# Expert stage of a graph and mixture-of-experts layer: opening with blocks listed from an early copy of the counts

## What is computed

```python
def gnn(x, adj, mask, W, b, a1, a2, att_b):
    h = x @ W + b
    att = sigmoid((h @ a1)[:, :, None] + (h @ a2)[:, None, :] + att_b) * adj * mask[:, :, None] * mask[:, None, :]
    att = att / (att.sum(-1, keepdims=True) + 1e-8)
    return (att @ h) * mask[:, :, None]

def ffn(x, gate_w, gate_b, w1, b1, w2, b2, gamma, beta):
    vals, idx = top_k(x @ gate_w + gate_b, 2)
    y_e = relu(x @ w1[e] + b1[e]) @ w2[e] + b2[e]          # for the two experts e of each token
    y = x + (softmax(vals) * y_e).sum()
    return layernorm(y) * gamma + beta

x = x + gnn(layernorm(x), ...)
x = x + ffn(layernorm(x), ...)
```

## Time and profile before

| | |
|---|---|
| median of 3 runs | 476.04 us (474.75 to 476.56) |
| the profiled execution, its own time | 477.23 us |
| span of the profiled execution | 475.5 us |
| busy: PE, DVE, ACT, POOL | 340.2, 313.2, 231.1, 324.4 us |
| scatters (L399), sends (L421) | 128 and 143 |
| first and last start of POOL's scatters | 48.28 and 211.60 us |
| first and last start of POOL's sends | 229.63 and 415.41 us |

### The profile page before, as it was taken

The page is one execution under the profiler, slowest core; times in us unless marked ns, Lnnn a source line. Parts: engine busy times, 40 slices in busy tenths (PEclk is TensorE's granted clock), DMA queues, the critical chain, the costliest instruction groups (busy, mean ns, idle before and its releaser), DMA issues.

```text
span 475.5 us, 11764 instructions
## 1 busy us (share of the span) xinstructions
PE 340.2 (72%) x2193; PEld 279.7 (59%) x2193; DVE 313.2 (66%) x1582; ACT 231.1 (49%) x608; POOL 324.4 (68%) x362
## 2 busy tenths in 40 slices
PE   2787988697778555103998989988889899058760
PEld 1666877687768454002877877777777788023220
DVE  3999898868968855701676666665555566118993
ACT  2767788788777364100333333333333335005663
POOL 6642777777777777660577777777777777705875
PEclk9998879969969955555999999999999999659995
DMA  7832445635444723595657777777777763179833
GB/s 206 280 106 63 146 157 173 203 110 210 158 156 156 266 102 111 178 257 178 200 163 223 234 206 228 218 216 219 220 223 226 210 197 103 37 277 291 274 108 110
DMA packets 61786, 87.96 MB, mean 185 GB/s; under 512 B 10343, under 2 KB 40973, under 8 KB 61604
## 3 DMA queue, kind: packets, MB, share of 16 engines
q1 hardware_dynamic: 32484, 44.87, 32.4%
q0 software_dynamic: 10720, 25.32, 14.8%
q10 hardware_dynamic: 18528, 17.19, 12.3%
HBM read 55.60 MB, written 32.72 MB: 186 GB/s over the span
## 4 chain that ended last, share of the span: by engine, by line
PE 24%; DVE 18%; ACTq 17%; issue 16%; ACT 9%; DMA 5%; POOL 5%; SPq 5%; DVEq 1%; POOLq 0%
PE psum L1190 6%; ACTq L553 6%; ACTq L272 5%; PE psum L1179 5%; ACTq L271 4%; ACT hid L558 4%; PE psum L1095 3%; DMA sorted_x<-xrow,rows 3%; PE psum L1113 3%; ACT z L582 3%; DVE st L654 2%; POOL sorted_x L399 2%; POOL token_y L421 2%; DVE xmid L718 1%; DVE rs L1010 1%
## 5 line engine op out<-in xcount | busy, mean ns | idle before, releaser
L421 POOL DMA_INDIRECT token_y<-yb,xb x143 | 143.4, 1003 | 60.4 <-issue 39.7
L399 POOL DMA_INDIRECT sorted_x<-xrow,rows x128 | 123.4, 964 | 42.0 <-issue 39.9
L558 ACT ACTIVATE hid<-psum,b_sb 128x256 f32<-128x256 f32 (+1 forms) x188 | 69.3, 419 | 140.4 <-PE psum L1179 63.4
L1190 PE MATMUL psum<-w_sb,hid 128*128 x572 | 83.3, 282 | 12.8 <-ACT hid L558 12.1
L1190 PEld LDWEIGHTS psum<-w_sb,hid 128*128 128x128 f32 x572 | 74.6, 191 | 22.4 <-issue 19.9
L1179 PE MATMUL psum<-xbT,w_sb 128*128 128x256 f32 (+1 forms) x376 | 81.9, 341 | 2.5 <-DVE xbT L955 2.2
L964 DVE TENSOR_TENSOR yb<-psum,b_bc 128x256 f32<-128x256 f32 x94 | 33.8, 360 | 63.1 <-PE psum L1190 50.2
L1179 PEld LDWEIGHTS psum<-xbT,w_sb 128*128 128x128 f32 x376 | 57.7, 193 | 8.2 <-DVE xbT L955 4.9
L969 DVE SCALAR_TENSOR_TENSOR yb<-yb,xb 128x128 f32<-128x128 f32 x143 | 46.6, 354 | 3.3
L1169 PE MATMUL psum<-ident_aug,xb 128*128 128x128 f32 x143 | 33.1, 288 | 21.8 <-DMA xb<-sorted_x 20.1
L955 DVE COPY xbT<-psum 128x256 f32<-128x256 f32 x94 | 33.2, 353 | 22.4 <-PE psum L1169 22.4
(11 more groups left out here) (159 smaller groups left out, 569.0 us busy)
## 6 DMA issues: line engine op xcount, KB each, us to landing
xb<-sorted_x SPq DMA_DIRECT2D x49, 258.0 KB
w_sb<-w_dram ACTq DMA_DIRECT2D x83, 128.0 KB
adj_in<-adj_dram SPq DMA_DIRECT2D x32, 256.0 KB
got<-token_y SPq DMA_DIRECT2D x16, 512.0 KB, 4.8
xb<-sorted_x SPq DMA_DIRECT2D x45, 129.0 KB
out_dram<-res ACTq DMA_DIRECT2D x16, 256.0 KB, 2.2
w_sb<-w_dram SPq DMA_DIRECT2D x27, 128.0 KB
xmid<-x_dram SPq DMA_DIRECT2D x6, 512.0 KB, 8.4
```

Source lines behind the costliest of these rows:

```text
L399: pool.indirect_dma_start(sorted_x, bass.IndirectOffsetOnAxis(ap=rows[:, slot, t, k:k + 1], axis=0), xrow[:, slot, k, t, :], None).then_in ...
L421: pool.indirect_dma_start(token_y, bass.IndirectOffsetOnAxis(ap=xb[:, q, t, TO:TO + 1].bitcast(I32), axis=0), yb[:, h, t, :], None, bounds ...
L558: last = act.activation(hid[:, u % RING, c, 0:n], psum[:, 2 + u % 2, c * BT:c * BT + n], ACT.Relu, bias=b1_sb[:, c, e])
L1190: last = mm(psum[:, 4 + u % 2, t * D:(t + 1) * D], hid[:, u % RING, c, t * P:(t + 1) * P], w2_sb[:, e, c * D:(c + 1) * D].rearrange("p a c ...
```

## The change

- The constants: `ORDER` is now 11 full units, then 15 times three one-tile units and a full one, then 23 full units. There are four lists of units: 17 full ones that lie wholly in what the first eight pairs wrote, 15 full ones of the middle, 17 full ones that are counted back from each expert's last row, and the 45 one-tile units.
- DVE copies `count` to `early` after the eighth pair. For this its loop is split: turns 4 to 9 in a loop, turns 10 and 11 written out with the copy between them, turns 12 and 13 in a loop of one pass.
- The table is computed from both copies: 44 operations on DVE from the fill copy to the last one, where there were 35, and then two copies into `tab` instead of one.
- POOL's setup has two memsets and four selects more for two columns of constants, one iota less, and its iota for the experts is 64 wide, not 16.
- SP issues, for the first 11 units, the row load and the weight load in turn, as soon as the table is there; the waits for fills and scatters come behind them. The first 11 units read rows of the first eight pairs alone.

The diff, cut to its core:

```diff
-FULL = (ITEMS - EXPERTS * (BT - 1)) // BT + 1
+EARLY_PAIRS = 8
+SPARE = EXPERTS * (BT - 1)
+EARLY = (EARLY_PAIRS * TPP * P * TOPK - SPARE - 1) // BT + 1
+LATE = (ITEMS - EARLY_PAIRS * TPP * P * TOPK - SPARE - 1) // BT + 1
+FULL = (ITEMS - SPARE - 1) // BT + 1
+MIDDLE = FULL - EARLY - LATE
 TAILS = (ITEMS - FULL * BT) // P + EXPERTS - 1
 UNITS = FULL + TAILS
-AHEAD = FULL - TAILS
-ORDER = tuple(range(AHEAD)) + tuple(b for i in range(TAILS) for b in (AHEAD + i, FULL + i))
-IN_RING = 11
+LISTS = 4
+FIRST_OF = (0, EARLY, EARLY + MIDDLE, FULL)
+IN_RING = OPENING = 11
+def woven(blocks, tails):
+    share = -(-len(tails) // len(blocks))
+    return tuple(u for i, b in enumerate(blocks) for u in tails[i * share:(i + 1) * share] + (b,)) + tails[share * len(blocks):]
+ORDER = (tuple(range(OPENING)) + woven(tuple(range(OPENING, EARLY + MIDDLE)), tuple(range(FULL, UNITS)))
+         + tuple(range(EARLY + MIDDLE, FULL)))
+assert EARLY == LATE and OPENING <= EARLY and sorted(ORDER) == list(range(UNITS)) and UNITS <= P
...
+            g.memset(unit_rows[:, :], float(P)).then_inc(unit_consts, 1)
+            g.memset(unit_list[:, :], 3.0 * EXPERTS).then_inc(unit_consts, 1)
+            pool.wait_ge(unit_consts, 2)
+            g.affine_select(out=unit_rows[:, :], in_=unit_rows[:, :], compare_op=ALU.is_ge, fill=float(BT), base=-FULL,
+                            pattern=[[0, 1]], channel_multiplier=1).then_inc(unit_consts, 1)
+            for l in (2, 1, 0):
+                pool.wait_ge(unit_consts, 5 - l if l < 2 else 2)
+                g.affine_select(out=unit_list[:, :], in_=unit_list[:, :], compare_op=ALU.is_ge, fill=float(l * EXPERTS),
+                                base=-FIRST_OF[l + 1], pattern=[[0, 1]], channel_multiplier=1).then_inc(unit_consts, 1)
...
-            sp.wait_ge(table_done, 1)
+            sp.wait_ge(table_done, 2)
...
-            for u in range(IN_RING):
+            for u in range(OPENING):
+                load_unit(u)
                 load_w1(sp, u)
             sp.wait_ge(filled, 16 * (EXPERTS + 1))
             sp.wait_ge(scattered[0], 16 * SCATTERS * PAIRS // 2)
             sp.wait_ge(scattered[1], 16 * SCATTERS * PAIRS // 2)
             sp.sem_inc(sp_passed, 1)
-            for u in range(UNITS):
+            for u in range(OPENING, UNITS):
                 load_unit(u)
...
+            def turns(lo, hi):
+                base = steps[0]
+                with dve.Fori(0, (hi - lo) // 2) as j:
+                    for s in range(2):
+                        steps[0] = base + j * (2 * per) + s * per
+                        turn(lo + 2 * j + s, (lo + s) % 2)
+                steps[0] = base + per * (hi - lo)
+            turns(LOOP_FROM, EARLY_PAIRS + 2)
+            turn(EARLY_PAIRS + 2, EARLY_PAIRS % 2)
+            dve.wait_ge(ranks_used, EARLY_PAIRS)
+            step(v.tensor_copy(early[:, :], count[:, :]))
+            turn(EARLY_PAIRS + 3, (EARLY_PAIRS + 1) % 2)
+            turns(EARLY_PAIRS + 4, LOOP_TO)
...
+            step(v.tensor_tensor(held[:, 0, :], early[:, :], first_row[:, :], ALU.subtract))
+            n = step(v.tensor_tensor(held[:, 1, :], count[:, :], early[:, :], ALU.subtract))
+            def whole_parts(k, bits, n):
+                dve.wait_ge(dve_step, n)
+                n = step(v.tensor_copy(cnt_i[:, 0:k, :], held[:, 0:k, :]))
+                dve.wait_ge(dve_step, n)
+                n = step(v.tensor_scalar(cnt_i[:, 0:k, :], cnt_i[:, 0:k, :], bits.bit_length() - 1, None, ALU.arith_shift_right))
+                dve.wait_ge(dve_step, n)
+                return step(v.tensor_copy(wide[:, 0:k, :], cnt_i[:, 0:k, :]))
+            def first_of(k, most, out, n):
+                dve.wait_ge(dve_step, n)
+                for l in range(k):
+                    n = step(v.tensor_tensor_scan(last_blk[:, l, :], ones_f[:, 0:EXPERTS], wide[:, l, :], 0.0,
+                                                  ALU.mult, ALU.add))
+                dve.wait_ge(dve_step, n)
+                n = step(v.tensor_tensor(excess[:, 0:k, :], wide[:, 0:k, :], last_blk[:, 0:k, :], ALU.subtract))
+                dve.wait_ge(dve_step, n)
+                n = step(v.tensor_scalar(excess[:, 0:k, :], excess[:, 0:k, :], float(most), 0.0, ALU.add, ALU.max))
+                dve.wait_ge(dve_step, n)
+                return step(v.tensor_tensor(out, excess[:, 0:k, :], wide[:, 0:k, :], ALU.min))
+            dve.wait_ge(unit_consts, 6)
+            n = whole_parts(2, BT, n)
+            n = first_of(2, EARLY, listed[:, 0:3:2, :], n)
...
+            step(v.scalar_tensor_tensor(out=start_row[:, 1, :], in0=listed[:, 0, :], scalar=float(BT), in1=first_row[:, :],
+                                        op0=ALU.mult, op1=ALU.add))
+            n = step(v.scalar_tensor_tensor(out=start_row[:, 2, :], in0=listed[:, 2, :], scalar=-float(BT), in1=count[:, :],
                                             op0=ALU.mult, op1=ALU.add))
             dve.wait_ge(dve_step, n)
-            n = step(v.tensor_scalar(blk[:, :, 1], blk[:, :, 4], -float(PAD_ROW), float(PAD_ROW), ALU.mult, ALU.add))
+            n = step(v.tensor_tensor(held[:, 0, :], start_row[:, 2, :], start_row[:, 1, :], ALU.subtract))
+            step(v.tensor_copy(start_row[:, 0, :], first_row[:, :]))
+            n = whole_parts(1, BT, n)
+            step(v.tensor_scalar(held[:, 1, :], held[:, 0, :], float(P - 1), None, ALU.add))
+            n = first_of(1, MIDDLE, listed[:, 1:2, :], n)
...
+            step(v.scalar_tensor_tensor(out=start_row[:, 3, :], in0=listed[:, 1, :], scalar=float(BT), in1=start_row[:, 1, :],
+                                        op0=ALU.mult, op1=ALU.add))
+            n = whole_parts(1, P, n)
             dve.wait_ge(dve_step, n)
-            n = step(v.tensor_tensor(blk[:, 0, 1:3], entry[:, 1, :], entry[:, 0, :], ALU.subtract))
+            n = step(v.tensor_copy(listed[:, 3, :], wide[:, 0, :]))
             dve.wait_ge(dve_step, n)
-            v.scalar_tensor_tensor(out=blk[:, 1, 0:2], in0=blk[:, 0, 1:3], scalar=blk[:, 0, 0:1], in1=entry[:, 0, :],
+            n = step(v.tensor_tensor_scan(last_unit, ones_f[:, 0:LISTS * EXPERTS], w_raw[:, 0:LISTS * EXPERTS], 0.0,
+                                          ALU.mult, ALU.add))
+            dve.wait_ge(dve_step, n)
+            n = step(v.tensor_scalar(past, last_unit, iota_p[:, :], None, ALU.is_le))
...
+            v.scalar_tensor_tensor(out=found[:, 6:7], in0=found[:, 4:5], scalar=found[:, 3:4], in1=found[:, 5:6],
                                    op0=ALU.mult, op1=ALU.add).then_inc(table_cols, 1)
             dve.wait_ge(table_ps, 1)
-            v.tensor_copy(tab[:, :], psum[0:1, 0, 0:2 * P]).then_inc(table_done, 1)
+            v.tensor_copy(tab[:, 0:P], psum[0:1, 0, 0:P]).then_inc(table_done, 1)
+            v.tensor_scalar(tab[:, P:2 * P], psum[0:1, 0, P:2 * P], float(EXPERTS - 1), None, ALU.min).then_inc(table_done, 1)
```

More of the change, by code:

```diff
@@ L862, in _ @@
             per = steps[0] - per
-            base = steps[0]
-            with dve.Fori(0, (LOOP_TO - LOOP_FROM) // 2) as j:
-                for s in range(2):
-                    steps[0] = base + j * (2 * per) + s * per
-                    turn(LOOP_FROM + 2 * j + s, (LOOP_FROM + s) % 2)
-            steps[0] = base + per * (LOOP_TO - LOOP_FROM)
+            def turns(lo, hi):
[11 more added lines that the diff above has]
+            turns(EARLY_PAIRS + 4, LOOP_TO)
             for m in range(LOOP_TO, PAIRS + 3):
@@ new lines, in _ @@
+            n = whole_parts(1, BT, n)
+            step(v.tensor_scalar(held[:, 1, :], held[:, 0, :], float(P - 1), None, ALU.add))
+            n = first_of(1, MIDDLE, listed[:, 1:2, :], n)
+            dve.wait_ge(dve_step, n)
+            n = step(v.scalar_tensor_tensor(out=held[:, 0, :], in0=listed[:, 1, :], scalar=-float(BT), in1=held[:, 1, :],
+                                            op0=ALU.mult, op1=ALU.add))
+            step(v.scalar_tensor_tensor(out=start_row[:, 3, :], in0=listed[:, 1, :], scalar=float(BT), in1=start_row[:, 1, :],
+                                        op0=ALU.mult, op1=ALU.add))
@@ new lines, in _ @@
+            dve.wait_ge(dve_step, m)
+            m = step(v.tensor_tensor(found[:, 4:5], found[:, 4:5], unit_rows[:, :], ALU.mult))
+            step(v.tensor_scalar(found[:, 5:6], found[:, 3:4], -float(PAD_ROW), float(PAD_ROW), ALU.mult, ALU.add))
+            step(v.tensor_tensor(found[:, 7:8], found[:, 0:1], unit_list[:, :], ALU.subtract))
+            dve.wait_ge(dve_step, m)
+            n = step(v.tensor_tensor(found[:, 4:5], found[:, 4:5], found[:, 2:3], ALU.add))
+            dve.wait_ge(dve_step, n)
```

113 lines of the change are left out of this document (38 added, 75 removed).

## The result

The changed kernel takes **481.79 us** (median of 4 runs, 479.14 to 483.51), the one before 475.94 beside it (4 runs, 474.75 to 476.56): ratio 1.0121, 95% interval [1.0067, 1.0175]. It is slower by 1.2%; 476.4 was forecast, with a range to 480.5. The profiled execution took 482.72 us about a span of 481.0.

A forecast was written before the change was run, and what follows sets the result against it. POOL's own pace, tied with ACT's queue, was taken to bound the kernel; 9.6 us gained at the opening are lost in the middle: last send +0.2, copy and loops 0.2, so 476.04 + 0.4 = 476.4 us, range 472.5 to 480.5.

The forecast's parts named there:

- What bounds the kernel: Expert stage: POOL at its own pace but for a 17.07 us hole, tied with ACT's queue, 3.92 against 3.90 us a pair.
- Rival B: Expert stage: POOL alone is the bound, last send ends 9.7 us earlier, 466.3 us; chance 0.08.
- Setup, copy, split loop, table: Before the expert stage: setup costs 0, copy and split loop 0.2 us, table at 203.5 costs 0.
- The first rows: Opening: x0 issued 12.7 us earlier, x1 in at 213, first send at 220 (217.7 to 222), 9.6 us of the hole go.
- From the first send to relu 10: Opening: unit 11's rows issued by SP at 231.0, landed at 233.6, so relu 10 at 235.0.
- Sixty intervals: Middle, relu 10 to 70: 1.93 us a unit on ACT, 115.8 in all, so relu 70 at 350.8.
- Rival D: Middle: ACT's queue slows through longer table reads, 2.00 us a unit, +4.2, 480.5 us; decides from 1.965; chance 0.17.
- C: Middle: ACT runs at its floor of 1.87 us a unit or just below, 472.7 us; chance 0.15.
- The rest: After relu 70: its send from 354.7, then 48 sends in 61.9 us, last send's end at 416.6; combine stage unchanged.
- Rival E: Opening: the early start does not come, first send 223 or after, 2 to 3 us lost, 479 us; chance 0.10.
- the ring of eleven: Load of unit 21 waits for unit 10's sends; just doesn't bind, but with a first send at 222 would, by 1.5 us.

The follow-up runs named there:

- e1: Changed kernel with the one-tile units spread evenly over the 38 full units behind the opening: 470.02 us, ratio 0.9872 to before.
- e3: Changed kernel, its order kept, with the layer 1 bias riding in the weight load and ACT's table read for it gone: 469.6 us, ratio 0.9871.
- e2: Changed kernel and order, but SP issues eleven weight loads and waits for fills and scatters before the first row load, as before: 489.56 us, ratio 1.0285.
- e5: Changed kernel with all 16 padding fills issued by ACT and none by SP: 483.0 us, ratio 1.0133 to before.
- f8: Changed kernel with even order, bias in the weight load, and SP's eight fills behind the loads of the first 11 units: 471.71 us, ratio 0.9907.
- f11: Changed kernel with SP's eight fills issued behind the loads of the first 11 units: 489.36 us, one run.
- h3: Changed kernel, its order kept, with twelve fills on ACT and four on SP behind the opening loads: 486.13 us, ratio 1.0254.
- h1: Changed kernel with even order, twelve fills on ACT and four on SP behind the opening loads: 472.22 us, ratio 0.9921.
- f7: Changed kernel with both the even order and the bias in the weight load: 469.74 us, ratio 0.9878 to before.
- g0: Changed kernel with one-tile units spread evenly, on a slower chip where before takes 625.06 us: 609.53 us, ratio 0.9782.

## Why the prediction was wrong, point by point

- *What bounds the kernel.* Right. POOL is at its own pace but for one hole, and ACT's queue is tied with it. e1, e3 and e2 each confirm a side of it: take the order or 0.43 us of ACT's queue away and the time falls by 12 us, leave both and undo the opening and it rises by 8. Rival B (POOL alone, 466.3) needs 1.3 us between the sends of the middle, and the trace of the changed kernel shows 1.0 to 1.9 us of waiting at each of the last ten full units of the middle. The Trainium skill, "Perfetto Trace Analysis", Identifying the Most-Contended Engine, takes occupancy for Scalar's headroom; the trace disagrees, with ACT at 48% and a read of 0.43 us less in its queue for each unit worth 12.2 us (481.79 to 469.6).
- *Setup, copy, split loop, table.* Right: the last scatter starts at 211.61 against 211.60, the table is there at 203.37 against 203.5.
- *The first rows.* **This is the step that failed.** The forecast had x1 in at 213 and the first send at 220, from the rate of SP's queue and 0.2 MB of fills left ahead; they were transposed at 215.45 and sent at 223.18, 1.2 us beyond the upper end of 222. Of the 3.2 us by which the first send was late, 2.45 lie in x1 and 0.7 between the transposes of unit 1 and the send (7.73 for 7.04). The sum by bytes had both its inputs nearly right, 0.25 MB left and 0.99 MB moved by 213; the mistake was to take x1 as landed when the queue had moved its bytes. Where SP's fills are not right ahead, unit 0's rows are transposed 2.8 to 4.0 us behind their issue (e2, e5, f8, f11, h3, h1) and unit 1's 3.1 to 5.8; where they are, 6.5 to 7.8 us (the changed kernel, e1, e3, f7) and 5.8 to 7.7. In e5 and h3 those fills run through ACT's queue at the same time. So it is the own queue, not the engines' load alone; and it takes a queue that has not drained, since g0 has the same fills right ahead and 2.75 us. The Trainium skill, "DMA: Bandwidth & Descriptors", Queues, rings and completion order, says that each DMA engine consumes the descriptors of a queue in the order of its ring. By it a load stands, on each engine, behind its issuer's earlier transfers there, and the trace agrees: the last fill packet starts at 211.24, and unit 0's rows are taken only at 213.17.
- *From the first send to relu 10.* **The second half of the same failure.** The forecast let relu 10 be set by SP's feed: unit 11 issued at 231.0, landed at 233.6, relu 10 at 235.0. SP was on time (231.26), but TensorE, busy without a break, came from a late start at 2.09 us a unit (relu 0 at 217.98, relu 10 at 238.88), and was at unit 11 only at 237.58. I had taken one of two chains without working out the other. Even with x1 in at 213, relu 0 would have been near 215.5 (2.5 us behind, as in the changed kernel) and relu 10, at 2.09 a unit, near 236.4, an estimate from these rows: so some 2.5 of the 3.9 us come from the late rows and 1.4 from the chain left out. This term is 3.9 of the 5.6 us by which the last send's end (422.2) missed 416.6.
- *Sixty intervals.* 1.93 was taken since single units ask less of TensorE and DVE; it was 1.948, the mean of before. The discount for small units had no ground, since the queue's length set the pace: +1.1 us. Rival D (1.965 and more) did not come, nor C.
- *The rest.* From relu 70 to its send 4.28 us in place of 3.9: +0.4. The 48 late sends 62.1 in place of 61.9: +0.2. The sum is 3.9 + 1.1 + 0.4 + 0.2 = 5.6 beyond the forecast. Against before the last send ends 5.8 us later; the combine stage behind it takes 58.8 against 59.1, so the spans differ by 5.5 and the medians by 5.85.
- *Rival E* had this case: "x1 waits behind fills", first send 223 or after, 479. It was the right mechanism at a chance of 0.10, and it counted 2 to 3 us by the ring of eleven, where the whole delay of relu 10 goes to the end. By the table above a relu 10 at 235.0 would have given an end of 418.3 and about 478.

**What stays open.** That SP's fills ahead of the loads cause the delay of relus 0 to 9 is shown (h3, f11). They do it in two ways: of the 4.9 us by which unit 1 is transposed earlier in f11, 2.5 are its earlier issue, since SP is not held up by the fills, and 2.4 its faster landing; in h3 3.0 and 1.5 of 4.5. That the DMA engines drift apart in the queue is read from packets and was not tested. That without the fills relu 10 would be at 235 is not, though relu 9 at 232.72 in h3 and another 2 us point there: each way of moving the fills made a new wait at or ahead of relu 10, on ACT (e5) or in the landing of the late fills (f8, f11, h3, h1). e3, f7 and e1 are the best versions found, 469.6, 469.7 and 470.0 us, 1.2 to 1.3% faster than before; with 1.305 us a send POOL is then the only bound.

## What to carry to other kernels

Cost every engine's queue as well as its compute: reads of registers and issues of DMAs are in no busy time, yet with a short part of the relus they made up the 1.95 us a unit that set this kernel's pace. When two engines are tied, keep in every stretch the mix of work that ties them; a reordering that suits one in one stretch and the other in the next costs the sum of both maxima, and what an earlier start brings is spent there first. When a load is moved forward, ask what its own issuer's queue still has ahead of it, and what the work it overtakes will now hold up when it lands. And don't take it as landed as soon as the queue has moved that many bytes.

## What the runs showed of the hardware

- A transfer of 258 KB issued behind eight fills of 129 KB in the same queue, 0.25 MB of which had still to move, was used 6.85 us after its issue; 3.1 us after it where the fills went through another queue (h3), and 2.75 where eight such fills were ahead in the same queue but had gone out over 19.8 us in place of 10.6 (g0).
- Packets of a later transfer started in that queue 3.7 us before the last packet of an earlier one (207.55 and 211.24 us).
- A table read into a register and what follows it took ACT's queue 0.28 + 0.15 us and the issue of a DMA 0.34, in no busy time.
- Four fills issued in a row behind the opening took 4.14 us from the last issue to landing, so a wait for them costs more than their issue.
- Two chips ran the same kernel in 470 (e1) and in 610 us (g0). In the stretches of the expert stage shown above TensorE's granted clock was 1.00 (2.4 GHz) on the one, where it was busy 117.67 of 134 us, and 0.87 on the other, a mix of its two levels of 1.2 and 2.4 GHz, where it was busy 84.34 of 118 us; a send cost 998 and 990 ns. The clock is not shown to be the cause. A bound found on one chip need not be the bound on the next.
